# A macaron transformer block on one core: the loop over twelve of the batches written out

## The reference

```
x = x + 0.5 * ffn(layernorm(x))
x = x + attention(layernorm(x))
x = x + 0.5 * ffn(layernorm(x))
```

## Time and profile before

| what | value |
|---|---|
| median of 3 runs | 2005.18 us (2001.39 to 2006.41) |
| profiled execution, its own time | 2006.59 us |
| its span in the profile | 2004.8 us |
| PE busy | 1820.8 us, 91% of the span |
| DVE, ACT, POOL busy | 1272.4, 988.0, 504.2 us |
| transfers | 99.79 MB |
| instructions | 29856 |

### The profile page before, as it was taken

How to read it: one execution, slowest core, us unless ns; L and a number is a source line. 1 busy time by engine, 2 the same in 40 slices (tenths; PEclk the granted TensorE clock), 3 DMA queues, 4 the chain that set the end, 5 groups by cost and what they waited for, 6 DMA issues and landing times.

```text
span 2004.8 us, 29856 instructions
## 1 busy us (share of the span) xinstructions
PE 1820.8 (91%) x9128; PEld 996.1 (50%) x9128; DVE 1272.4 (63%) x2795; ACT 988.0 (49%) x1954; POOL 504.2 (25%) x663
## 2 busy tenths in 40 slices
PE   6598999999899998999989999899989999998885
PEld 4344545454454645455454545446445464545244
DVE  5476767676566765667657676666747676764631
ACT  1246554546555453555535555454545545464541
POOL 1404142131413213141311414122141422313101
PEclk9698999999999998999989999999989999999797
DMA  4504124050501405032240503206050140605000
GB/s 108 96 13 78 26 44 74 12 106 12 100 8 43 74 12 106 12 70 37 43 75 12 106 3 71 45 12 106 12 104 4 45 72 12 106 1 102 5 12 11
DMA packets 96817, 99.79 MB, mean 50 GB/s; under 512 B 19974, under 2 KB 88327, under 8 KB 96519
## 3 DMA queue, kind: packets, MB, share of 16 engines
q1 hardware_dynamic: 93896, 97.19, 26.1%
q10 hardware_dynamic: 2752, 0.54, 0.2%
HBM read 63.54 MB, written 33.55 MB: 48 GB/s over the span
## 4 chain that ended last, share of the span: by engine, by line
PE 63%; DVE 9%; DMA 9%; issue 8%; ACT 4%; SPq 3%; POOL 2%; POOLq 0%; DVEq 0%; ACTq 0%
PE ps L520 10%; PE ps L508 9%; PE ps L496 8%; PE ps L587 8%; PE ps L566 6%; DMA scratch<-parts 5%; DVE mx L838 5%; PE ps L575 4%; PE ps L624 4%; SPq L481 3%; DMA out_dram<-x 3%; PE ps L642 3%; PE ps L687 2%; ACT pr L722 2%; PE ps L627 2%
## 5 line engine op out<-in xcount | busy, mean ns | idle before, releaser
L838 DVE TENSOR_REDUCE mx<-ps 128x1 f32<-128x512 f32 x1024 | 655.2, 685 | 277.4 <-PE ps L496 274.6
L722 ACT ACTIVATE pr<-ps 128x512 f32<-128x512 f32 x1024 | 555.9, 598 | 288.1 <-PE ps L508 287.6
L496 PE MATMUL ps<-stack 96*128 96x512 bf16 x1024 | 329.2, 391 | 59.8 <-issue 36.4
L508 PE MATMUL ps<-stack 98*128 98x512 bf16 x1024 | 322.7, 387 | 18.6 <-ACT pr L722 9.8
L520 PE MATMUL ps<-pr,va 128*32 128x512 f32 x2048 | 275.2, 610 | 4.6 <-ACT pr L722 4.6
L777 ACT ACTIVATE h<-ps,benc 128x512 f32<-128x512 f32 x128 | 88.0, 687 | 254.8 <-PE ps L566 254.8
L508 PEld LDWEIGHTS ps<-stack 98*128 98x128 bf16 x1024 | 77.7, 100 | 271.3 <-ACT pr L722 174.1
L496 PEld LDWEIGHTS ps<-stack 96*128 96x128 bf16 x1024 | 97.4, 99 | 221.9 <-DVE mx L838 88.1
L890 DVE SCALAR_TENSOR_TENSOR ps<-ps,wb,h 128x512 f32<-128x512 f32 x128 | 96.7, 756 | 138.4 <-PE ps L575 138.4
L1035 POOL TENSOR_SCALAR rs<-mv 128x4 f32<-128x4 f32 x48 | 11.2, 232 | 646.1 <-DVE mv L858 640.4
L575 PE MATMUL ps<-h,gram_w 128*128 128x512 f32 x256 | 132.5, 599 | 0.0
(11 more groups left out here) (155 smaller groups left out, 2983.9 us busy)
## 6 DMA issues: line engine op xcount, KB each, us to landing
stack<-scratch SPq DMA_DIRECT2D x384, 128.0 KB, 4.4
scratch<-parts SPq DMA_DIRECT2D x64, 384.0 KB, 5.6
xin<-in_L_attn_x_dram SPq DMA_DIRECT2D x16, 512.0 KB, 3.5
out_dram<-x SPq DMA_DIRECT2D x16, 512.0 KB, 6.1
stack<-wu_mT SPq DMA_DIRECT2D x128, 4.0 KB, 1.7
cst<-in_const_dram SPq DMA_DIRECT2D x1, 1024.0 KB
raw<-in_L_ffn_W_dec_dram ACTq DMA_DIRECT2D x1, 512.0 KB, 5.8
pr<-in_L_ffn_W_enc_dram SPq DMA_DIRECT2D x2, 256.0 KB, 7.8
```

The lines of the kernel that those rows point to most:

```text
L496: pe.matmul(bank1[:, t % 2, :], stack[b.odd][0][0:KB, hd, 128 * t:128 * t + 128], stack[b.odd][1][0:KB, hd, :], start=True, stop=True).the ...
L508: pe.matmul(bank2[:, a % 2, :], stack[b.odd][1][:, 4 * g + a, 128 * t:128 * t + 128], stack[b.odd][0][:, 4 * g + a, :], start=True, stop=T ...
L722: act.activation(pr[:, n % 2, a, :], bank2[:, a % 2, :], ACT.Exp, scale=SCALE).then_inc(ex_done.sem, 1)
L838: dve.tensor_reduce(mx[:, hd // 4 % 2, e:e + 1], bank1[:, t % 2, :], AX.X, ALU.max).then_inc(mx_done.sem, 1)
```

## The change

The loop in `walk` is gone, and all eighteen iterations are emitted by `known`, with the batch's number as an integer. So there is no branch, every wait is for a constant, and the addresses of load and store are constants. The order of the work within each iteration, the buffers and the semaphores are the same. GpSimd still reads the chosen adapter's number into a register in each batch.

```diff
-    for i in (-1, 0, 1):
-        known(i)
-    trips = (B - 4) // 2
-    with engine.Fori(0, trips) as k:
-        one(2, k * 2 + 2, 0)
-        one(3, k * 2 + 3, 1)
-    for i in range(2 + 2 * trips, B + 1):
+    for i in range(-1, B + 1):
         known(i)
```

## The result

The changed kernel takes 1970.64 us (median of 4 runs, 1970.11 to 1971.88), the kernel before beside it 2005.80. The ratio is 0.9829, 95% interval 0.9812 to 0.9846: 35 us faster, inside the range of 1956 to 1977, and 7.6 us above the 1963 that was forecast. The profiled execution took 1970.23, against 2006.59 before.

What follows compares the result with a forecast made beforehand. TensorE sets the end, busy 91% of the span, with pauses at the loop's taken branches on its chain. Gains of 40.4 + 1.9 + 0 + 0 = 42.3 us from 2006.59, less 1.4 to the median, gave 1963; range 1956 to 1977.

Steps and rivals of the forecast that it cites:

- Five taken branches: At the loop's seams: five windows with a taken branch become like nine without, losing 40.4 us, 8.1 each.
- The sum: Whole kernel: 40.4 + 1.9 + 0 + 0 = 42.3 us gained, for a time of 1963 us.
- Fetching the longer program: Instruction fetches: the loop's code is already fetched anew each trip, so the longer program costs 0 more.
- The late-fetch rival: TensorE's written-out instruction stream: late blocks cost 7.4 us or more each, 2052 us with twelve; chance 0.03.
- must be removed together to gain: At the loop's branch: ScalarE stands still 7.2 us beside TensorE's 7.6, so sparing only one gains nothing.
- The store: At seams without a pause: VectorE's addition waits for the store, about 14 times instead of nine, 2 to 3 us each.
- Its address: SyncE's store at the seam: a constant address issues it up to 0.16 us earlier, twelve times, 1.9 us.
- Register waits: TensorE's and VectorE's sequencers: 23.8 and 30.2 us of register instructions go, hidden, gain 0; rival on the path 1939, chance 0.04.
- The clock: TensorE: granted clock 1.00 in every window; the rival, sinking under load, loses 19 us, time 1982, chance 0.03.
- The rival of the seams at their slowest: At the seams: all twelve windows take 115.71 us, a gain of 28.5, time 1977; chance 0.07.

Runs made afterwards that it cites:

- the three loop kernels: All engines loop, in six trips (the kernel before), three or two, with five, two or one taken branches: 2006.0, 1988.7 and 1976.1 us.
- locked at 10.7: Changed kernel plus 119 already-met waits an iteration on TensorE, 79 in the first batch, holding its fetch 10.0 to 11.3 us before the seam's transposes: 1961.65 us.
- the trips: Against the kernel before, all engines loop in three trips of four iterations or two of six, with register waits in the same twelve iterations: 1988.68 and 1976.13 us.
- the padding: Changed kernel plus 115 already-met waits an iteration on TensorE, and 0, 27, 81 or 156 at the start: 1962.65, 1962.46, 1973.70, 1983.62 us.
- locked at 20.2: Changed kernel plus 119 already-met waits an iteration on TensorE and 74 at the start, fetch 20.1 to 20.3 us before the seam's transposes: 1992.59 us.

## Why the prediction was right, and where not

**Five taken branches, 40.4 us.** Right in kind and in cause. With the loop on TensorE alone the whole gain is lost; on ScalarE alone, nothing. The size was right as well: the five windows that had a branch lost 41.5 us together, 8.3 each, against the 40.4 forecast. Outside the seam it is plain to see in one iteration, 3, before and after the change (the body of the iteration, columns as in the earlier trace rows):

```profile
433.50:549.04 115.54, 104.77 (x545) 56.36 (x544) 73.90 (x166) 60.27 (x121) 31.25 (x41) 0.98 0.28 52
435.50:543.37 107.87, 104.33 (x545) 56.12 (x544) 73.39 (x166) 57.55 (x113) 29.77 (x36) 1.00 0.24 42
```

The 34.4 / 5 = 6.9 us a branch in the stretch is lower because it is net of what the seven other windows lost, 7.1 us together, and the 7.1 a branch over the three loop kernels has such losses in it too. The sum had these seven stay as they were. I had no ground for that but the mean of nine windows without a branch, and seven of those nine lay inside the loop, where each taken branch starts the fetching anew, so that TensorE's fetches fell at the same two places in each trip, about 17.6 and 10.5 us before the transposes, both harmless. The one in written-out code with all the work, 115.71, had its fetch at 20.1 us and a first write of 3.4; it was in the earlier trace rows as the slowest, and I took its length for scatter. Locked at 10.7 us, the written-out kernel has its twelve windows in 1374.87; the forecast had 1416.99 - 42.3 = 1374.7.

**The 7.7 us between the changed kernel and the one locked at 10.7.** They are the difference of the two stretches, 1382.59 and 1374.87. Measured against the mean of 114.57 of the locked kernel's windows: the three windows with a slow first write (115.65, 116.46, 115.83) are 4.2 us long, the one with the sunken clock (117.14) 2.6, three with a slow transfer of maxima (115.03, 114.81, 115.48) 1.6, and the other five together 0.7 short. The sunken clock followed a seam that a slow first write had made late. The maxima are the same mechanism at another place: at 968.25 SyncE issues a pair, a fetch falls into it, and TensorE waits 1.2 us for it (the waits of TensorE, 971 to 974 us, in the changed kernel):

```profile
PE ps L502 <- DMA stack<-wu_mT: 1.2, 1, 1.2
```

**Fetching the longer program, 0.** This is the step of the sum that failed. Its count was right and generous (73 fetches, not 83), but a count was the wrong measure. What a fetch costs hangs on where it falls, from nothing to some 1.9 us at one seam (116.46 against 114.57). The late-fetch rival asked only for pauses of 7.4 us in TensorE's own stream, and none came. The Trainium skill, "Runtime: NRT & Kernel Launch", section "Instruction fetch mechanics", has long kernels stream their instructions in blocks of 256 with the cost mostly hidden; the trace agrees for TensorE itself, which in the twelve windows was never idle for more than 2.1 us at a time, and then for VectorE's maxima, and doesn't for the transfers beside it.

**ScalarE.** I wrote that its pauses and TensorE's "must be removed together to gain". That was read off the branch's line alone and is wrong: ScalarE's pause, 5.8 to 6.9 us in the kernel that loops there alone, lies where nobody waits for it.

**The store.** Late next, as said: 14 waits, 34.8 us. **Its address, 1.9 us:** the gap from the landing of the third write to the issue of the store was 2.97 us in the loop (1719.57 + 5.56 to 1728.10) and is 2.74 (1453.26 + 5.77 to 1461.77) now, 0.23 less for the 0.16 expected. The kernel before had 2.73 in its own iteration 1, which is written out. That all of it reaches the end wasn't measured by itself. **Register waits, 0:** right, by the trips, the padding and the bodies of the iterations. **The clock:** 1.00 in eleven of twelve windows; it sank once, from a late seam, not from load.

The rival of the seams at their slowest (twelve times 115.71, 1977 us) stood for the part that came true in four windows of twelve.

That the time fell inside the range is in part luck. Where the fetches fall wasn't in the forecast, and by that alone a written-out kernel can take 1992.59 us, padded and locked at 20.2, well outside the range. The changed kernel has its fetches wandering, and so hit the first write in only three windows of twelve.

That the fetch and the write meet on the same DMA engine is likely, by the eight late packets of 128 (there are 16 engines), and not shown: the trace doesn't say which engine carried a packet. The fetches of the four other engines (60 of 8 KB on the queue q14) weren't moved. Moving the write, or its place in SyncE's queue, wasn't tried.

## What to carry to other kernels

When a loop is written out, look at two things: whose branch really stops someone, best by keeping the loop on one engine at a time, and where the instruction fetches of the engine with the most instructions fall afterwards. A window that is one or two microseconds longer than its neighbours is not scatter until the DMA view of it has been compared with theirs. Where a short transfer sits on the path in each iteration, waits that are already met, added where the sequencer runs ahead, can hold the fetches away from it; here 119 of them an iteration cost nothing that could be seen. The kernel with them has the lowest median measured, 1961.65 us, 6.3 below the changed kernel beside it, and three others are within 2.5 us of it.

## What the runs showed of the hardware

A taken branch of the loop of six trips stops TensorE for 6.7 to 7.9 us here, ScalarE for 5.8 to 7.2 and VectorE for 4.8 to 5.5, while GpSimd and SyncE, with far fewer instructions in a trip, go on within 0.3 us. With two or three trips it is 4.9 to 6.6 us on TensorE, 4.3 to 5.6 on ScalarE and 3.5 to 4.8 on VectorE. Only on TensorE does the pause stand in the branch's own record; on the others it is the gap to the next instruction. One fetch of 16 KB stretched a write of 384 KB from 2.3 to as much as 4.3 us, and one of 4 KB from 1.7 to 3.7. Two kernels that differ only by 74 waits at the start, and by them in the place of the fetches in every iteration, differed by 28 us, 1.4% (1964.15 and 1992.59).
